# Attention values weighed for two key units in succession, with six probability buffers

## What is computed

```python
x = x + 0.5 * ffn(layernorm(x))      # layer 1
x = x + attn(layernorm(x))
x = x + 0.5 * ffn(layernorm(x))      # layer 2, the same weights

def attn(x):                         # 16 heads of width 8, rotary positions
    q, k, v = heads(x @ Wq.T), heads(x @ Wk.T), heads(x @ Wv.T)
    q, k = rope(q), rope(k)
    score = where(causal, q @ k.T, -inf)          # 1024 x 1024 per head
    return merge(softmax(score / sqrt(8)) @ v) @ Wo.T

def ffn(x):                          # 8 experts, the best one per token
    probs = softmax(x @ Wr + br); idx = argmax(probs); gate = max(probs)
    xn = normalised(x) * ln_g + ln_b
    return gate * (relu(xn @ W1[idx] + b1[idx]) @ W2[idx] + b2[idx])
```

## Time and profile before

| | us |
|---|---|
| median of 3 runs | 932.06 (926.17 to 937.27) |
| profiled execution, device time | 934.51 |
| its span, first to last instruction | 932.7 |
| busy: TensorE / VectorE / ScalarE / GpSimd | 770.6 / 633.5 / 556.0 / 352.5 |
| mean granted clock of TensorE | 0.911 of 2.4 GHz |

### The profile page before, as it was taken

One profiled execution on the slowest core, in us unless ns is written; L12 is line 12 of the kernel. 1 busy time (PEld: TensorE's weight loads), 2 busy tenths in 40 slices (PEclk: granted clock), 3 DMA queues, 4 the chain that ended last, 5 costly groups with the idle time before them and its releaser, 6 DMA issues. The chain is left out here.

```text
span 932.7 us, 16893 instructions
## 1 busy us (share of the span) xinstructions
PE 770.6 (83%) x5318; PEld 416.8 (45%) x5318; DVE 633.5 (68%) x1750; ACT 556.0 (60%) x1196; POOL 352.5 (38%) x635
## 2 busy tenths in 40 slices
PE   9578884287289999999999999999999989488784
PEld 7477774144013333333333333333333329477774
DVE  4645663599587887788787787778778306656663
ACT  2078883144126667676667766776767563178883
POOL 5077762078411332233222332233223310177762
PEclk9589998599559999999999999999999779589997
DMA  9821220325740210222022211221020000521120
GB/s 313 179 53 50 50 45 8 91 78 141 196 99 2 52 41 13 53 52 53 7 48 53 53 23 31 53 53 37 17 53 2 2 16 18 97 52 51 49 45 8
DMA packets 41267, 54.51 MB, mean 58 GB/s; under 512 B 8019, under 2 KB 33757, under 8 KB 39776
## 3 DMA queue, kind: packets, MB, share of 16 engines
q1 hardware_dynamic: 33680, 42.99, 19.4%
q0 software_dynamic: 4992, 9.44, 4.2%
q10 hardware_dynamic: 2512, 1.06, 0.5%
HBM read 36.19 MB, written 17.79 MB: 58 GB/s over the span
## 5 line engine op out<-in xcount | busy, mean ns | idle before, releaser
L1341 DVE CUSTOM_DVE_ANT_0 cst<-psS,cst 128x768 bf16<-128x768 f32 (+7 forms) x512 | 364.2, 755 | 103.3 <-PE psS L1215 100.6
L1305 ACT ACTIVATE prob<-psST 128x512 f32<-128x512 f32 (+3 forms) x768 | 323.8, 496 | 141.8 <-PE psST L1240 138.6
L1254 PE MATMUL a_psO<-prob,vs 128*32 128x512 f32 (+3 forms) x1536 | 167.6, 509 | 0.9 <-POOL prob L1426 0.7
L1425 POOL TENSOR_TENSOR a_gate<-a_zeros 1x1 f32<-1x1 f32 x128 | 23.4, 183 | 334.4 <-ACT prob L1305 334.4
L1240 PE MATMUL psST<-a_qs,ks 75*128 75x512 bf16 (+1 forms) x480 | 124.0, 327 | 5.6 <-ACT prob L1305 3.3
L1215 PE MATMUL psS<-ks,a_qs 72*128 72x512 bf16 (+2 forms) x480 | 116.5, 332 | 5.3 <-DVE a_rowmax L1341 5.2
L761 POOL DMA_INDIRECT f_row<-rows,f_there_number x78 | 77.6, 996 | 102.3 <-DMA rows<-tok 79.2
L1215 PE MATMUL psS<-ks,qs 72*128 72x512 bf16 (+3 forms) x288 | 76.6, 360 | 24.4 <-DMA qs<-q_split 17.1
L647 PE MATMUL f_ps_wide<-f_xnT,f_w1s 128*128 128x128 f32 x624 | 86.6, 284 | 2.2 <-ACT f_xnT L711 2.2
L1240 PE MATMUL psST<-qs,ks 75*128 75x512 bf16 (+3 forms) x288 | 79.6, 349 | 6.5 <-ACT prob L1305 5.4
L647 PEld LDWEIGHTS f_ps_wide<-f_xnT,f_w1s 128*128 128x128 f32 x624 | 79.5, 200 | 3.3 <-ACT f_xnT L711 3.3
(11 more groups left out here) (154 smaller groups left out, 983.6 us busy)
## 6 DMA issues: line engine op xcount, KB each, us to landing
ks<-k_split SPq DMA_DIRECT2D x48, 192.0 KB
a_qs<-q_split SPq DMA_DIRECT2D x60, 96.0 KB
k_split<-p_part SPq DMA_DIRECT2D x40, 128.0 KB, 2.3
rows<-tok SPq DMA_DIRECT2D x8, 524.0 KB, 9.3
qs<-q_split SPq DMA_DIRECT2D x36, 96.0 KB
q_split<-p_part SPq DMA_DIRECT2D x24, 128.0 KB, 2.3
w<-in_Wb SPq DMA_DIRECT2D x1, 2064.0 KB, 7.5
w<-in_W SPq DMA_DIRECT2D x1, 2048.0 KB, 12.6
```

The costliest lines, as they stand in the source:

```text
L1254: last = nc.tensor.matmul(psO[32 * h:32 * h + 32, c0:c0 + w], vs[r][:, j, h, :], prob[:, u % RING, h, 0:w], start=(j == 0), stop=(u + 1 in ...
L1305: nc.scalar.activation(prob[:, u % RING, h, 0:w], psST[(u * QH + h) % 3][:, 0:w], ACT.Exp, scale=SCALE).then_inc(exp_done, 1)
L1341: last = nc.vector.tensor_tensor_reduce(out=out[:, a * CH:a * CH + width], in0=ps[:, a * CH:a * CH + width], in1=mask_row[:, S - width:], ...
```

## The change

- `plan` puts weighings only behind head 0 of the odd units (GROUP = 2), and then two: units u - 3 and u - 2. Behind unit 1 these are units 10 and 11 of the stage before.
- There are PRING = 6 probability buffers. Three are the old ones; `lent` makes views of the same size in the memory of `n.w1` and `n.w2`, of which three are used (`w` in the rows). ScalarE waits for the weighing of six units earlier instead of three.
- `copy_out` comes ahead of unit 2 (it was 1) and of unit 6 (it was 5); `turn_out` of half 0 comes behind unit 6 (it was 5).
- The experts' weights are overwritten during attention, so layer 2 loads them again (`load_experts`, three DMAs on SyncE behind that of the table), and VectorE and ScalarE wait for them there.

No matmul, tile or exponential is added or removed.

```diff
@@ -43,6 +43,7 @@
 WARM = (30, 16)
 GATHER_AHEAD = 10
 RING = 3
+PRING, GROUP = 6, 2
 
 
 FIRST_ROOT = float(0x5f3759df)
@@ -214,16 +215,22 @@
                   n.x[b].rearrange("(n p) d -> p n d", p=P)).then_inc(n.x_loaded[b], 16)
 
 
-LOADS = 5
+EXPERT_LOADS, LOADS = 3, 5
 
 
 def load_weights(sp, n):
 
     for b in range(B):
         sp.wait_ge(n.x_loaded[b], 16)
+    load_experts(sp, n)
+    for there, source in ((n.cst[:, HEAD_W:], n.const[:, HEAD_W:]), (n.wproj[:, :, :], n.Wp)):
+        sp.dma_start(there, source).then_inc(n.weights_loaded, 16)
+
+
+def load_experts(sp, n):
+
     for there, source in ((n.w1[:, :, :], n.Wb1), (n.w2[:, :, 0:FB * D], n.W2),
-                          (n.w2[:, :, FB * D:], n.b2.partition_broadcast(P)),
-                          (n.cst[:, HEAD_W:], n.const[:, HEAD_W:]), (n.wproj[:, :, :], n.Wp)):
+                          (n.w2[:, :, FB * D:], n.b2.partition_broadcast(P))):
         sp.dma_start(there, source).then_inc(n.weights_loaded, 16)
 
 
@@ -502,8 +509,7 @@
             choose()
             positions()
             dve.wait_ge(experts_known, 1)
-            if r == 0:
-                dve.wait_ge(n.weights_loaded, 16 * LOADS)
+            dve.wait_ge(n.weights_loaded, 16 * (LOADS + r * EXPERT_LOADS))
 
             def first_weights(t, k):
 
@@ -693,8 +699,7 @@
             act.wait_ge(n.table_loaded, 16)
             nc.scalar.activation(tile_number[:, 0, :, :], tile_is, ACT.Copy, scale=n.c("partition")).then_inc(low_made, 1)
             act.wait_ge(experts_known, 1)
-            if r == 0:
-                act.wait_ge(n.weights_loaded, 16 * LOADS)
+            act.wait_ge(n.weights_loaded, 16 * (LOADS + r * EXPERT_LOADS))
 
             def normalise(t, k):
                 if there(t):
@@ -742,6 +747,8 @@
             sp.dma_start(table[:, :].bitcast(U16), n.tables16).then_inc(table_read, 16)
             if r == 0:
                 load_weights(sp, n)
+            else:
+                load_experts(sp, n)
             sp.wait_ge(rows_ready, 3)
             for b in range(B):
                 sp.dma_start(n.rows_dram[r][b * S:(b + 1) * S, :].rearrange("(n p) d -> p n d", p=P),
@@ -806,6 +813,9 @@
 
     with ExitStack() as ctx:
         n.prob = ctx.enter_context(nc.sbuf_tensor("prob", [P, RING, QH, CH], F32))
+        lent = [w[:, :, :].rearrange("p e w -> p (e w)")[:, i * QH * CH:(i + 1) * QH * CH]
+                .rearrange("p (h c) -> p h c", h=QH) for w in (n.w1, n.w2) for i in range(2)]
+        n.prob_ring = ([n.prob[:, i, :, :] for i in range(RING)] + lent)[:PRING]
         n.psST = [ctx.enter_context(nc.psum_tensor(f"psST{i}", [P, CH], F32)) for i in range(3)]
         n.psS = [ctx.enter_context(nc.psum_tensor(f"psS{i}", [P, 2 * CH], F32)) for i in range(2)]
 
@@ -1088,13 +1098,14 @@
             for h in range(QH):
                 found.append(("score", u, h))
                 att += w
-                if h == 0:
-                    if u >= LAG:
-                        found.append(("weigh", u - LAG, 0))
-                        att += WEIGH_COST * units[u - LAG][3]
-                    elif not first:
-                        found.append(("weigh", u - LAG, 1))
-                        att += WEIGH_COST * units[u - LAG + UN][3]
+                if h == 0 and u % GROUP == LAG - 1:
+                    for v in range(u - LAG - GROUP + 1, u - LAG + 1):
+                        if v >= 0:
+                            found.append(("weigh", v, 0))
+                            att += WEIGH_COST * units[v][3]
+                        elif not first:
+                            found.append(("weigh", v, 1))
+                            att += WEIGH_COST * units[v + UN][3]
                 spread()
             for at, what, arg, there in EXTRAS:
                 if at == u and (there or not (first if arg == 1 and what == "turn_out" else last)):
@@ -1110,7 +1121,7 @@
     LAG = 2
     AHEAD = tile_total * tile_cost[0]
 
-    EXTRAS = [(1, "turn_max", 1, True), (4, "turn_out", 1, False), (5, "turn_out", 0, True),
+    EXTRAS = [(1, "turn_max", 1, True), (4, "turn_out", 1, False), (6, "turn_out", 0, True),
               (7, "turn_max", 0, False)]
     before_loop = [(0, "tile", t) for t in range(MT // 2)] + [(0, "turn_max", 0)]
     before_loop += [(0, "tile", t) for t in range(MT // 2, MT)]
@@ -1139,7 +1150,11 @@
     qs = n.qs + [sb(f"qs{i}", [PR + MR, QH * S], BF16) for i in range(1, RING)]
     ks, vs = n.ks, n.vs
     MP = KINDS * QH * CB
-    prob, psST, psS = n.prob, n.psST, n.psS
+    psST, psS = n.psST, n.psS
+
+    def prob(s, u):
+        return n.prob_ring[(s * UN + u) % PRING]
+
     rowmax = sb("rowmax", [P, QH, TB])
 
 
@@ -1289,8 +1304,8 @@
             else:
                 turn_max(0, arg, k, psS[k % 2])
         run(stage)
-        weigh(NST - 1, (NST - 1) % RING, UN - 2)
-        weigh(NST - 1, (NST - 1) % RING, UN - 1)
+        for u in range(UN - GROUP, UN):
+            weigh(NST - 1, (NST - 1) % RING, u)
         end = base(NST - 1, False) + len(uses(False, True))
         turn_out(NST - 1, 1, end, psS[end % 2])
 
@@ -1299,10 +1314,10 @@
         def exps(s, u):
 
             ch, j, q0, w = units[u]
-            wait(act, pv_done, s * UN + u - 2)
+            wait(act, pv_done, s * UN + u - PRING + 1)
             for h in range(QH):
                 act.wait_ge(scored, s * SC + u * QH + h + 1)
-                nc.scalar.activation(prob[:, u % RING, h, 0:w], psST[(u * QH + h) % 3][:, 0:w], ACT.Exp,
+                nc.scalar.activation(prob(s, u)[:, h, 0:w], psST[(u * QH + h) % 3][:, 0:w], ACT.Exp,
                                      scale=SCALE).then_inc(exp_done, 1)
 
         def copy_out(s, ch):
@@ -1312,9 +1327,9 @@
 
         def stage(s, r, turn, first, last):
             for u in range(UN):
-                if u == 1 and not first:
+                if u == LAG and not first:
                     copy_out(s - 1, 1)
-                if u == half_end[0] + 1:
+                if u == half_end[0] + LAG:
                     copy_out(s, 0)
                 exps(s, u)
...
```

More of the change, by code:

```diff
@@ L1254, in weigh @@
                 last = nc.tensor.matmul(psO[32 * h:32 * h + 32, c0:c0 + w], vs[r][:, j, h, :],
-                                        prob[:, u % RING, h, 0:w], start=(j == 0),
+                                        prob(s, u)[:, h, 0:w], start=(j == 0),
                                         stop=(u + 1 in half_end))
@@ L1422, in mask @@
             pool.wait_ge(exp_done, s * SC + (u + 1) * QH)
-            part = prob[:, u % RING, :, 0:P]
+            part = prob(s, u)[:, :, 0:P]
             nc.gpsimd.tensor_tensor(gate[:, u:u + 1], zeros[0:1, 0, 0:1], zeros[0:1, 0, 1:2], ALU.add)
```

## The result

The changed kernel takes 1049.98 us (median of 4 runs, 1047.79 to 1063.98), the kernel before in the same comparison 934.66 (926.17 to 939.33): ratio 1.124, interval 1.113 to 1.135. The forecast was 996 with a range to 1040. The direction is right, the time is 54 us too low, and it lies outside the range. Some executions of every kernel run at a lower granted clock and take longer; ratios and intervals here leave these out, so a ratio can differ a little from the quotient of the two medians.

What follows compares the result with a forecast made beforehand. TensorE was taken to bound attention, by its work and program order. To 934.5 us the prediction added 57.6 (fifteen stages), 1.6 and 2.5 (last stage) and 0 (buffers, copies, second load): 996, range 955 to 1040.

Steps and rivals of the forecast that it cites:

- What bounds the kernel: Attention block: TensorE bounds by total work, 28.89 of 30.30 us per stage; its program order decides whether VectorE keeps up.
- the second load: Layer 2 loading the experts again: landed by 785 to 790, first read at 810.84, so cost 0.
- The pairs' gain: Attention stages: two weighings in one go save 0.19 us per pair (0 to 0.23), 18 us over 96 pairs.
- The hand-run: New TensorE order followed through a stage: stalls make the period 34.14 instead of 30.30 us, 57.6 in fifteen stages.
- Copies: Output copies one unit later: ScalarE's wait removed, price in units 2 and 6 counted in the hand-run, 0 beside it.
- Buffers: Six probability buffers, three in the experts' memory: only loosen a ScalarE wait, cost and gain 0.
- The clock in the stages: Fifteen attention stages with tiles: no fall of TensorE's clock inside them, so nothing for it in the 57.6 us.
- rival 3: Clock falls in half of the attention stages, 2.6 to 6 us each, 20 to 45 us: 1016 to 1040; chance 0.30.
- The rule of the page: Skill section on the clock, as read: it falls only with long idle gaps, so by it alone 996 would stand.
- The last stage: Last attention stage, without tiles: 1.6 us for four pairs plus 2.5 us for a longer low-clock stretch.
- Rivals 1 and 2: Attention: pairs' gain stays, 916, chance 0.06; or half the stalls, 1 to 2.5 us per stage, 950 to 975, chance 0.15.
- the planner's burst: Behind each pair the planner emits two tiles, a score, a third tile; in units 4 and 5 the third stalls 0.84 us.

Runs made afterwards that it cites:

- e1: Changed kernel with weighings one by one, copies and turns as before; six buffers and second load kept: 928.38 us against 925.73 before, ratio 1.000.
- e4: Changed kernel with the next score product repeated one to four times at six stalling places, 16 repeats per full stage: 1003.23 us, ratio 1.083 to before.
- e5: e4 with the output copies and the turn of half 0 back where before has them: 1051.03 us against 983.92 before, ratio 1.068.
- e2: Changed kernel with at most one tile between two other items of TensorE's order: 1049.37 us, ratio 1.132 to before.
- e9: Changed kernel with VectorE's maxima over only the last 128 keys of each tile: 992.65 us against 993.92 before, ratio 1.001.
- e10: e3 with the next score product repeated one or two times ahead of five stalling items: 1035.12 us against 993.92 before, ratio 1.043.
- e3: Changed kernel with weighings counting nothing in the planner's account, so tiles spread over scores alone: 985.08 us, ratio 1.064 to before.
- e6: Changed kernel with units 4 to 9 weighed singly, other pairs kept, copies and turns as before: 1004.38 us against 983.92 before, ratio 1.019.

## Why the prediction was wrong in its size

The failed step is that stages with the new order were taken to keep the clock at 1.00. The steps in their order:

- **What bounds the kernel** was right: the order of TensorE's program, through banks that VectorE and ScalarE free. e1 excludes the buffers and the second load.
- **The pairs' gain** was slightly too low. A single weighing costs 0.31 + 1.00 from the score ahead of it to the next product, two 2.62; the pair with its approach costs 0.31 + 1.86 and one more score of 0.22, that is 2.39. So 0.23, the upper end, 22 us in all, if the small pairs give as much.
- **The hand-run** held. It gave a period of 34.14; at full clock it is 34.25 in the changed kernel and 34.35 with the repeats (e4). That e5 gives 34.14 exactly is chance, since its copies stand elsewhere. The half with small tiles takes 14.76 us (510.39 to 525.15, 2.79 ahead of the pair) against 14.65; the half with large tiles, where both falls of the clock are, 22.75 against 19.49. Two weak points had no effect: the check on before at 448.56 was none, because the 1.30 us come from that very row, and the stalls named for the first half (1.98 less a gain of 0.57) don't add up to its 0.77.
- **Copies** cost 0.2 us per stage (34.35 against 34.14), 3 us in all; the hand-run had a stall of 0.61 for one of them. Buffers 0 (e1) and the second load 0 (26 us to spare): right.
- **The clock in the stages** is the step that failed. The forecast put it at nothing in the 57.6 us, and rival 3, which priced it, had a chance of 0.30 and falls "in half of the stages, 20 to 45 us". The clock was at half speed twice in each of the last eleven stages with tiles, and for up to 17 us between two copies of the output in the four ahead of them. The 15 stages lost 108.9 us; the order is 15 times 4.05, 60.8 of them, and 48 are the clock, a little above rival 3's range. With the start 7.8 too late and the last stage 5.2 better than forecast that is the 54 us.
- **The size of a fall** was off in two ways that cancelled in part. The stretch is 3.4 us in the steady stages, not 7 to 16. Each microsecond at half speed costs 0.46 to 0.49 (two stretches 3.3 us, from 34.25 to 37.54), not 0.38; the 0.38 rests on a busy share of 78%, for which no row stands, and the stage at full clock is busy 85% (29.12 of 34.25), with which the same working gives 0.44. And there were about two falls per stage instead of half a one. That rival 3's sum comes near 48 is luck.
- **The evidence for it** was there: the hand-run had TensorE streaming 2.3 of 4.2 us behind the first pair, and the earlier trace rows a fall behind a stretch busy 73%. But it was not decisive. Measured as those rows are, that stretch of the trace (492.29 to 496.51) is busy 2.74 of 4.22 us, 65%, and yet this order, with the same waits of 0.68 and 0.70, passed one stage without a fall. The forecast could not have known that the clock would fall every time; its fault was to hold rival 3 to half of the stages, so that the range ended at 1040.
- **The rule of the page.** By the Trainium skill, TensorE: Matmul & The Clock Gate, HAM oscillation, I had put the fall down to long idle gaps. Here no wait of TensorE from 320 to 720 us was over 0.7 us, and the clock fell twice in every stage but the first four. The measurement decides against that reading, and the reading was mine: the section speaks of long gaps, and I took it to say that short waits are harmless.
- **The last stage** had the wrong sign: −1.1 instead of +4.1. Its clock was 0.87 on average where it had been 0.75 in before, as the windows show, before and after:

```profile
731.70:767.00 35.30, 30.35 (x173) 8.70 (x173) 2.44 (x9) 21.61 (x52) 7.93 (x23) 0.75 0.00 1
```
```profile
849.00:882.50 33.50, 26.79 (x171) 8.76 (x170) 2.41 (x9) 20.58 (x51) 7.54 (x22) 0.87 0.01 2
```

Before had its long fall already in this stage; a fall there was no surcharge of the change.
- **Rivals 1 and 2** (gain kept, half the stalls) are excluded by e4 and by the change's own stage at full clock: 4.05 and 3.95 us are lost.
- **What I thought was the mechanism of the stall,** the planner's burst, is not: e2 takes it away and gains next to nothing. VectorE and ScalarE run dry during 1.9 us, and their few banks do not let TensorE give the work back faster than they do it. 2.6 of the 4.05 us go with VectorE's work (e9), and 1.5 with where the tiles stand (e10 against e4); the two overlap, and ScalarE's part is argued.

Left open: how the 1.5 us per stage beyond VectorE divide, why pair 2/3 costs where pair 10/11 gains, and why the clock falls in one stage and not in the next of the same order. What e4 loses beyond 15 times 4.05 stands in its trace: the first distance between copies is 44.75 us, 17.1 of them at half speed, and one later is 36.0, with 3.4.

## What to carry to other kernels

When an in-order engine feeds others through a few banks, a long piece of work on it costs them what outlasts their backlog, even when all are below 80% busy; compare the length of the piece with the banks' worth of work before counting the switches that it saves. Look for places where the busy share of TensorE drops in every turn of a loop: the clock may then fall in every turn (e3), in some (e10, four of 15) or in none, so price the case in which it always falls and let the range reach it. To separate clock from order, fill the stalls with repeated products and read the period again.

## What the runs showed of the hardware that I had not expected

- The clock falls with short waits. Ahead of the two stretches at 0.50 TensorE was busy 2.50 and 2.32 of 3.30 us, none of its waits over 0.7 us; sixteen repeats of 0.22 us per stage held it at 1.00 for 380 us.
- The falls can lock to the loop. e3 has a period of 34.13 and one stretch at half speed in each, the change, from its fifth stage on, 37.5 and two, stage after stage. But they need not: e10 falls in four stages of 15, e6 in three, and the change itself passes one without.
- 3.4 us at half speed cost about 1.6 us of the period in these stages: 1.55 in e10, 1.6 in e6, 1.65 in e4, half of 3.3 in the change.
- Entering and leaving the weighings' product form costs 0.23 us together, by the distances between starts: a pair with its approach takes 2.39 us, two single weighings 2.62.
- The same kernel before has medians of 926 to 935 us on some chips and 984 and 994 on two others, with a maximum over 1024 keys at 1.22 us on each.
